# Routing tiles transposed by DMA during the readout, early gathers and weight loads in the routing block, query transposes on TensorE

## The chip, the cores and the metric

One core of one Trainium2 chip runs the whole program in one launch. The metric is the time of one execution on the device, in microseconds (us). Engines: TensorE (PE; PEld is its weight load), VectorE (DVE), ScalarE (ACT), GpSimd (POOL) and SyncE (SP). SP issues nearly all DMAs, POOL the casting and the indirect ones; 16 DMA engines move the data.

## The reference

The layer is a chain of four residual updates on x, shape (4, 512, 512), that is 2048 tokens of 512 features, with a context of (4, 1024, 512).

```python
x = x + tanh(g_xattn[0]) * xattn0(layernorm(x), ctx, mask)   # softmax(x ctx^T) ctx
x = x + tanh(g_ffn[0])   * ffn0(layernorm(x), router_w, wg, wu, wd)
x = x + tanh(g_xattn[1]) * xattn1(layernorm(x), ctx, Wq, bq, Wk, bk, Wv, bv, Wo, bo)   # 16 heads
x = x + tanh(g_ffn[1])   * ffn1(layernorm(x), w1, b1, w2, b2)   # 8 experts by position
```

`ffn0` picks for each token one of 8 experts by the argmax of 8 router logits. Each expert is three 512x512 products with ternary weights and with activations rounded to 8 bits: `down(square(relu(gate(x))) * up(x))`. The change touches the part between the end of the first update and the queries of the third.

## The kernel before, in words

The program is a row of blocks, each with one instruction list per engine; a block ends when every engine has finished its list, and the next one begins behind that barrier. Tokens are held as 16 tiles of 128 (`NT = 16`), four to a batch (`QD = 4`). A value of float32 precision is carried through TensorE as a pair of bf16 tiles, high and low part. "Turning" a pair means transposing its two 128x512 halves into eight 128x128 blocks, so that features lie on the partitions.

**Readout** (`readout_phase`, about 250 to 439 us): for each tile TensorE makes the scores of a later tile and the weighted sum of an earlier one. SP turns the pairs of x (L489) and of the probabilities (L495) by DMA transposes. From tile 5 on, DVE and ACT also do the routing work that does not need a finished batch ("route" of eleven tiles, `ROUTED_EARLY = 11`): the normalised tile is split into high (ACT, L541) and low part (DVE, L623) and quantised (ACT, L543) into a dispatch row.

**Routing** (`router_phase`, about 439 to 485 us): POOL zeroes a tile (L788), computes the reciprocal deviations (L789 to L791) and the padding (L792, L793), issues eight casting loads of the experts' ternary weights (L795), and then writes constants. SP loads the router's weights, then stores the dispatch rows to DRAM: eleven tiles when POOL's padding and DVE's first coefficients are there (L822), the other five when DVE and ACT have made them (L825, L827); it waits for the landing at L828 and L829. DVE normalises the five late tiles, TensorE turns all 16 tiles (L986) into PSUM, ACT copies each to SBUF (L845), TensorE makes the logits (L994). From the logits DVE (L915 to L975) computes each token's expert, and the list `token_of` (L968) that says which token stands in which row of 23 expert tiles.

**Mixture** (`mixture_phase`, to about 576 us): SP first loads the query and output weights (L1269). POOL gathers each expert tile's rows from DRAM (L1065) by `token_of`, four buffers deep; TensorE turns them (L1186) and runs the three products (L1202, L1217).

**Query** (`query_phase`, about 578 to 676 us): POOL gathers the mixture's rows back (L1331). Per batch DVE adds them (L1418), normalises four tiles (L1434, after POOL's deviations at L1337) and makes the low parts (L1439); ACT makes the high parts (L1394); SP turns the pairs by DMA (L1365); TensorE makes 4 groups of 12 matmuls (L1477); ACT (L1400) and DVE (L1444) take them out of PSUM, and SP stores them (L1373). SP's list is in this order: four pieces of the query weights and eight tiles turned; 32 loads of keys and values (L1251, L1254) for the attention block; then per batch four stores and four turns. The output weights are turned last. Attention follows at 676 us.

Of the kernel before, what the change touches and what calls it, by code (L numbers as in the profile page):

```python
# [6 lines left out]
F32 = mybir.dt.float32  # L7
# [409 lines left out]
RW = 2 * D + DW  # L417


def routed_views(flat):  # L420

    v = flat[:, 0:ROUTED_SHARED * RW].rearrange("p (t w) -> p t w", w=RW)
    return v[:, :, 0:2 * D].rearrange("p t (r d) -> p t r d", r=2), v[:, :, 2 * D:]


def readout_phase(nc, sem, mask, gates, ident, ctxN, ctxT, xres, moments, amax, routed):
# [4 lines left out]
    with ExitStack() as c:  # L431
# [19 lines left out]
        xpairs, disp = routed_views(routed)  # L451
# [28 lines left out]
        with nc.Block() as block:  # L480
            @block.sync
            def _(sp):
# [38 lines left out]
            def _(act):  # L521
# [15 lines left out]
                def route(r):  # L537
# [3 lines left out]
                    nc.scalar.copy(xpairs[:, r, 0, :], rxn[r % 2]).then_inc(rhi_done, 1)  # L541
# [18 lines left out]
            def _(dve):  # L560
# [43 lines left out]
                def route(r):  # L604
# [18 lines left out]
                    v.tensor_tensor(xpairs[:, r, 1, :], xn_r, xpairs[:, r, 0, :], ALU.subtract).then_inc(rlo_done, 1)  # L623
# [73 lines left out]
def router_phase(nc, sem, router_w, wt_dram, means, ident, xres, moments, amax, routed, wT, scales, expert_of, token_of, place, dispatch_dram):  # L697
# [5 lines left out]
    with ExitStack() as c:  # L703
# [9 lines left out]
        q32 = sb("r_q32", [P, 2, D], F32)  # L713
# [26 lines left out]
        chain = sem("r_chain")  # L740
# [37 lines left out]
        with nc.Block() as block:  # L778
            @block.gpsimd
            def _(pool):  # L780
# [6 lines left out]

                done(nc.gpsimd.memset(rows[:, :], 0.0))  # L788
                done(nc.gpsimd.memset(half[:, :], -0.5))  # L789
# [42 lines left out]
            def _(act):  # L832
# [8 lines left out]
                def x_copy(t):  # L841
                    act.wait_ge(xposed, t + 1)
                    if t >= 2:
# [5 lines left out]
                x_copy(0)  # L849
                act.wait_ge(router_xposed, 1)  # L850
                nc.scalar.copy(rT[:, :, :], psR[:, :, 0:E]).then_inc(router_ready, 1)
                for t in range(1, NT):
                    x_copy(t)
                    late = ROUTED_EARLY + (t - 3) // 2
                    if t >= 3 and t % 2 == 1 and late < NT:
                        high(late)
                        integers(late)

            @block.vector
            def _(dve):  # L860
# [107 lines left out]
                then(v.tensor_copy(token_of[:, :], psI))  # L968
# [1637 lines left out]
```

## Time and profile before

| | |
|---|---|
| time, median of 3 runs | 1586.51 us (1579.5 to 1591.86) |
| the profiled execution's own time | 1584.77 us |
| its span in the trace | 1583.0 us |
| TensorE busy, share of the span | 87% |
| VectorE | 70% |
| ScalarE | 57% |
| GpSimd | 33% |
| mean granted TensorE clock | 0.928 |

Times in rows are microseconds from the start of the span. A busy share is a mean over blocks that have different limits, so each block is read from its own stretch. "Idle before <- X" in a row names what the engine's idle time ended with.

### The profile page before, as it was taken

Reading aid. Unit: us, or ns where it says so; the run is one execution under the profiler, and the core shown is the slowest. Engines: PE = TensorE matmul, PEld = TensorE weight load, DVE = VectorE, ACT = ScalarE, POOL = GpSimd, SP = SyncE. Lnnn points to the kernel's source line nnn. Section 1 sums busy time; section 2 is a strip of 40 time slices with the busy share of each in tenths; the row PEclk is TensorE's granted clock in tenths of the full one; section 3 lists DMA queues with packets and bytes.
Section 4 is the critical chain, followed back from the end, with each engine's and each line's share of the span. In section 5 each row is a group of like instructions: output and inputs, shape, how many; then the busy total and the mean of one; then the engine's idle time right before and its main releaser. Section 6 shows DMA issues by size and latency. Waiting matters only on the chain. (4 is left out here: it accounts for less than half of the span.)

```text
span 1583.0 us, 25515 instructions
## 1 busy us (share of the span) xinstructions
PE 1369.5 (87%) x9345; PEld 813.7 (51%) x9415; DVE 1113.4 (70%) x1442; ACT 897.0 (57%) x1384; POOL 518.5 (33%) x412
## 2 busy tenths in 40 slices
PE   6899996999855945579999999999786999999996
PEld 4455552444342512216677777774233666666663
DVE  6888856677755968387888787875677766555561
ACT  7878842333353832307777777777434866656550
POOL 0122210000032324029999999997510000000000
PEclk9999998999966978759999999999897999999998
DMA  6888762533274459903353535352464965765540
GB/s 233 285 272 297 255 220 74 100 74 70 51 301 172 130 149 188 242 23 62 65 108 66 108 67 106 69 169 59 149 212 154 328 199 196 238 229 198 206 140 25
DMA packets 237166, 248.98 MB, mean 157 GB/s; under 512 B 121692, under 2 KB 154591, under 8 KB 236040
## 3 DMA queue, kind: packets, MB, share of 16 engines
q1 hardware_dynamic: 231224, 221.49, 49.2%
q0 software_dynamic: 5840, 26.14, 4.8%
q8 instruction: 63, 1.03, 0.3%
q14 instruction: 39, 0.32, 0.1%
HBM read 169.62 MB, written 52.59 MB: 140 GB/s over the span
## 5 line engine op out<-in xcount | busy, mean ns | idle before, releaser
L1726 POOL TENSOR_TENSOR t_low<-t_e 128x1024 bf16<-128x1024 f32 x185 | 365.1, 2003 | 47.7 <-ACT t_e L1773 47.6
L1811 DVE TENSOR_REDUCE t_nmax<-t_psM 128x1 f32<-128x1024 f32 x256 | 309.5, 1221 | 74.8 <-PE t_psM L1894 73.0
L1773 ACT ACTIVATE t_e<-t_psE 128x512 f32<-128x512 f32 x512 | 277.9, 595 | 104.5 <-PE t_psE L1916 97.3
L1894 PE MATMUL t_psM<-kst,qst 96*64 96x512 bf16 x1024 | 188.6, 405 | 13.9 <-DVE t_nmax L1811 7.0
L2435 PE MATMUL e_psG<-late_flat,e_w1p 128*128 (+1 forms) x1536 | 174.1, 277 | 13.1 <-DVE e_hT L2379 8.4
L1916 PE MATMUL t_psE<-qst,kst 99*64 99x512 bf16 x1024 | 181.7, 385 | 1.3
L2435 PEld LDWEIGHTS e_psG<-late_flat,e_w1p 128*128 128x128 bf16 x1536 | 152.2, 99 | 35.3 <-DVE e_hT L2379 8.0
L1930 PE MATMUL t_psO<-t_e,vst 128*33 128x512 bf16 x768 | 163.8, 391 | 3.7 <-POOL t_low L1726 3.7
L2450 PE MATMUL e_psO<-e_w2p,e_hT 128*128 128x512 bf16 x752 | 164.9, 379 | 0.8
L1894 PEld LDWEIGHTS t_psM<-kst,qst 96*64 96x64 bf16 x1024 | 88.8, 113 | 77.9 <-DVE t_nmax L1811 35.2
L2450 PEld LDWEIGHTS e_psO<-e_w2p,e_hT 128*128 128x128 bf16 x768 | 75.2, 98 | 88.8
L1930 PE MATMUL t_psO<-t_low,vst 128*33 128x512 bf16 x384 | 115.0, 380 | 0.0
L1916 PEld LDWEIGHTS t_psE<-qst,kst 99*64 99x64 bf16 x1024 | 80.6, 108 | 59.2 <-ACT t_e L1773 45.0
L120 POOL DMA_DIRECT2D ternary<-c_wout x48 | 41.8, 870 | 174.0 <-ACT c_wout L241 174.0
L669 PE MATMUL a_psS<-ctxT,a_xT 128*128 128x512 bf16 x375 | 86.6, 386 | 13.7 <-DMA a_xT<-a_xpair 13.0
L1477 PE MATMUL q_psG<-late_flat,q_wqT 128*128 128x512 bf16 x188 | 44.6, 398 | 53.9 <-DMA late_flat<-q_pair 50.9
L2331 ACT CAST e_w2p<-xres 128x2048 bf16<-128x2048 f32 x32 | 60.7, 1898 | 52.9 <-PE e_psO L2450 31.2
L376 PE MATMUL c_psG<-ctxT,c_wT 128*128 128x512 bf16 x369 | 86.6, 383 | 4.6 <-issue 2.7
L2337 ACT ACTIVATE e_g<-e_psG,e_b1T 128x256 f32<-128x256 f32 x128 | 53.6, 470 | 63.6 <-PE e_psG L2435 38.8
L1930 PEld LDWEIGHTS t_psO<-t_e,vst 128*33 128x33 bf16 x768 | 76.4, 109 | 23.1 <-POOL t_low L1726 4.7
L379 PE MATMUL c_psG<-c_wT,ctxT 128*128 128x512 bf16 x371 | 87.0, 384 | 0.7
L2371 DVE TENSOR_TENSOR e_w1p<-piece,e_w1p 128x2048 bf16<-128x2048 f32 x32 | 72.2, 2287 | 18.2 <-ACT e_w1p L2326 18.2
(270 smaller groups left out, 2212.7 us busy)
## 6 DMA issues: line engine op xcount, KB each, us to landing
piece<-in_L_ffn_w SPq DMA_DIRECT2D x32, 1024.0 KB, 13.9
xres<-in_L_ffn_w SPq DMA_DIRECT2D x32, 1024.0 KB, 15.2
wT<-ternary POOLq DMA_DIRECT2D x8, 1536.0 KB, 24.1
kst<-keys SPq DMA_DIRECT2D x96, 128.0 KB, 3.5
c_rows<-in_ctx SPq DMA_DIRECT2D x8, 1024.0 KB, 8.8
xres<-in_L_ffn_wg SPq DMA_DIRECT2D x8, 1024.0 KB, 6.0
xres<-in_L_ffn_wu SPq DMA_DIRECT2D x8, 1024.0 KB, 7.9
xres<-in_L_ffn_wd SPq DMA_DIRECT2D x8, 1024.0 KB, 6.4
```

Of the source, the lines that this page charges most:

```text
L376: last = nc.tensor.matmul(psG[:, k, :], wT[:, 0, a, k * P:(k + 1) * P], ctxT[:, b, q * 512:(q + 1) * 512], start=(i == 0), stop=(i == 11))
L379: last = nc.tensor.matmul(psG[:, k, :], ctxT[:, a, q * 512 + k * P:q * 512 + (k + 1) * P], wT[:, 1, b, :], start=(i == 0), stop=(i == 11))
L669: last = nc.tensor.matmul(psS[:, par, h * 512:(h + 1) * 512], xT[:, par, ra * KC + k, :], ctxT[:, rb * KC + k, bass.ds(b * T + h * 512, 512)],
L1726: nc.gpsimd.tensor_tensor(low[:, low_slot(h, u), :, :], e32[:, slot(h, u), :, :], upper(h, u), ALU.subtract).then_inc(lo_pool, 1)
L1773: nc.scalar.activation(e32[:, slot(h, u), i, :], psE[:, i, :], ACT.Exp, scale=SC).then_inc(expd, 1)
L1811: nc.vector.tensor_reduce(nmax[:, h // G % 2, h % G, u:u + 1], banks_of(place_of_max(b, m)).rearrange("p a t -> p (a t)"), AX_X, ALU.max, ...
L1894: last = nc.tensor.matmul(banks_of(place_of_max(b, m))[side * SIDE:(side + 1) * SIDE, i, :], qst[0:KR, g, h % G, s0:s0 + SIDE], kst[0:KR, ...
L1916: last = nc.tensor.matmul(psE[side * SIDE:(side + 1) * SIDE, i, :], kst[:, g, h % G, t0:t0 + SIDE], qst[:, g, h % G, :], start=True, stop= ...
L1930: return nc.tensor.matmul(psO[side * SIDE:side * SIDE + VW, h % 2, :], values(i, r), part[:, i, :], start=first, stop=last)
L2371: nc.vector.tensor_tensor(half1(1, p), raw1(p), half1(0, p), ALU.subtract).then_inc(w1_lo, 1)
L2435: last = nc.tensor.matmul(psG[:, g % 4, i, :], w1p[:, ra, k, f:f + P], xeT[:, rb * KC + k, ee, :].rearrange("p o s -> p (o s)"), start=(n ...
L2450: last = nc.tensor.matmul(psO[:, m, :], hT[:, ra, k, m * P:(m + 1) * P], w2p[:, rb, k, :], start=(k == 0 and i == 0), stop=(k == FC - 1 an ...
```

## The change

- The eleven early tiles are turned in the readout: their pairs now go into two buffers, and SP turns them by DMA (`turn_routed`) into the place where the pairs stood. ACT waits before it writes a pair's buffer until the turn of two tiles earlier has landed. In the routing block TensorE turns only the five late tiles, and ACT copies only those.
- POOL issues four of the eight weight loads directly behind its first memset, ahead of the deviations and the padding; the other four stay where they were.
- POOL issues the mixture's first four gathers at the end of the routing block, once the dispatch rows have landed and `token_of` is there. Their buffers share memory with the quantised tiles.
- In the query block all turns are done by TensorE into PSUM, eight transposes for one pair, and ACT copies the result to SBUF. TensorE's list holds one pair's transposes behind each group of 12 matmuls. SP's loads of keys and values wait for the first batch's update alone.

```diff
@@ readout_phase
+                def turn_routed(r):
+                    sp.wait_ge(rlo_done, r + 1)
+                    sp.dma_start_transpose(turned_of(rturned, r), rpairs[r % 2].rearrange("p r d -> p (r d)")).then_inc(r_turned[r % 2], 16)
...
                     if t + 1 < NT:
                         turn_p(t + 1)
+                    if 0 <= t - 6 < ROUTED_EARLY:
+                        turn_routed(t - 6)
+                turn_routed(ROUTED_EARLY - 1)
+                for i in range(2):
+                    sp.wait_ge(r_turned[i], (ROUTED_EARLY + 1 - i) // 2 * 16)
...
-                    nc.scalar.copy(xpairs[:, r, 0, :], rxn[r % 2]).then_inc(rhi_done, 1)
+                    if r >= 2:
+                        act.wait_ge(r_turned[r % 2], r // 2 * 16)
+                    nc.scalar.copy(rpairs[r % 2][:, 0, :], rxn[r % 2]).then_inc(rhi_done, 1)
@@ router_phase, POOL
                 done(nc.gpsimd.memset(rows[:, :], 0.0))
+                for e in range(E // 2):
+                    fetch(e)
                 done(nc.gpsimd.memset(half[:, :], -0.5))
...
-                for e in range(E):
-                    nc.gpsimd.dma_start(wT[:, e, :, :, :, :].rearrange("p m r k d -> p (m r k d)"),
-                                        wt_dram[e].rearrange("p m r k d -> p (m r k d)")).then_inc(w_fetched, 16)
+                for e in range(E // 2, E):
+                    fetch(e)
...
+                pool.wait_ge(early_stored, 16)
+                pool.wait_ge(late_stored, 32)
+                pool.wait_ge(q_cast, NT - ROUTED_EARLY)
+                pool.wait_ge(token_ready, 1)
+                for j in range(4):
+                    nc.gpsimd.indirect_dma_start(m_rows[:, j, :].bitcast(F32), None, dispatch_dram[:, :],
+                                                 bass.IndirectOffsetOnAxis(token_of[:, j:j + 1], 0)).then_inc(m_loaded[j], 16)
                 pool.wait_ge(w_fetched, 16 * E)
@@ router_phase, ACT
-                x_copy(0)
+                high(ROUTED_EARLY)
+                integers(ROUTED_EARLY)
                 act.wait_ge(router_xposed, 1)
                 nc.scalar.copy(rT[:, :, :], psR[:, :, 0:E]).then_inc(router_ready, 1)
-                for t in range(1, NT):
-                    x_copy(t)
-                    late = ROUTED_EARLY + (t - 3) // 2
-                    if t >= 3 and t % 2 == 1 and late < NT:
-                        high(late)
-                        integers(late)
+                for t in range(ROUTED_EARLY + 1, NT):
+                    high(t)
+                    integers(t)
+                    x_copy(t - 1)
+                x_copy(NT - 1)
@@ router_phase, TensorE
                 for t in range(NT):
-                    if t + 1 < NT:
+                    if t + 1 >= ROUTED_EARLY and t + 1 < NT:
                         x_transposes(t + 1)
                     judge(t)
@@ query_phase, SP
-                for n in range(NWT + 2 * QD):
-                    turn(n)
+                sp.wait_ge(updated, QD)
                 prefetch(sp)
...
-                    if b + 2 <= B:
-                        for k in range(QD):
-                            turn(NWT + (b + 2) * QD + k)
@@ query_phase, ACT
-                for n in range(NWT + 2 * QD):
+                for n in range(NWT):
+                    split(n)
+                    if n >= 2:
+                        copy(n - 2)
+                copy(NWT - 2)
+                copy(NWT - 1)
+                for n in tiles_of(0):
+                    split(n)
+                for n in tiles_of(0):
+                    copy(n)
+                for n in tiles_of(1):
                     split(n)
...
                         evacuate(b, k)
+                        copy(NWT + (b + 1) * QD + k)
                         if b + 2 <= B:
                             split(NWT + (b + 2) * QD + k)
@@ query_phase, TensorE
                     if m == 0:
-                        for i in range(4):
-                            pe.wait_ge(turned[i], (b + 2) * 16)
+                        pe.wait_ge(copied, NWT + (b + 1) * QD)
...
+                for n in range(NWT):
+                    transposes(n)
+                for n in tiles_of(0):
+                    transposes(n)
                 for b in range(B):
                     for m in range(KC):
                         gemm(b, m)
+                        transposes(NWT + (b + 1) * QD + m)
```

## Rows read from the trace of the kernel before

**Rows 1.** Busy time by stretch, readout: length, then each engine's busy time (count), clock, DMA.

```profile
300.00:325.00 25.00, 24.89 (x115) 11.37 (x116) 16.52 (x26) 7.61 (x11) 1.48 (x2) 1.00 0.44 82
```

**Rows 2.** Readout's transposes: timeline (start, length), then issues with us to landing.

```profile
394.08 33.33 SPq L495 DMA_TRANSPOSE a_pT<-a_ppair  x4
...
405.22 0.62 ACT L541 CAST late_flat<-ctxT 128x512 bf16<-128x512 f32 x1 [1.75 <-DVE ctxT L610]
...
437.53 0.75 DVE L597 SCALAR_TENSOR_TENSOR xres<-a_psR,a_coef,xres 128x512 f32<-128x512 f32 x1 [1.87 <-PE a_psR L681]
...
a_xT<-a_xpair SPq DMA_TRANSPOSE x16, 3.0
```

**Rows 3.** Timeline of the routing block, and of its groups of instructions the costliest.

```profile
440.10 0.11 POOL L789 MEMSET r_half<- 128x16 f32 x1
...
443.79 4.35 POOL L795 DMA_DIRECT2D wT<-ternary  x8
...
460.95 0.69 DVE L883 TENSOR_TENSOR r_xpair<-r_xn,r_xpair 128x512 bf16<-128x512 f32 x1 [2.17 <-ACT r_xpair L835]
...
466.63 0.29 DVE L915 TENSOR_REDUCE r_top<-r_psL 128x16 f32<-128x128 f32 x1 [4.45 <-PE r_psL L994]
...
480.80 0.18 DVE L968 CAST token_of<-r_psL 128x23 int32<-128x23 f32 x1
...
L845 ACT COPY r_xT<-r_psX 128x1024 bf16<-128x1024 bf16 x16 | 15.8, 1032 | 2.3 <-PE r_psX L986 2.3
```

**Rows 4.** DMA queues in 440:446, then 464:466 (packets, MB, share); SP's issue and wait.

```profile
q1 hardware_dynamic: 331, 0.34, 19.7%
...
q0 software_dynamic: 66, 0.76, 91.8%
q1 hardware_dynamic: 60, 0.06, 11.7%
...
462.63 0.48 SPq L827 DMA_DIRECT2D dispatch<-r_disp  x1
...
SPq L829 <- DMA dispatch<-r_disp: 21.6, 1, 21.6
```

**Rows 5.** Timeline at the start of the mixture block.

```profile
486.50 1.07 POOL L1065 DMA_INDIRECT m_rows<-dispatch,token_of  x1 [33.53 <-DVEq L1172]
...
490.40 0.95 POOL L1065 DMA_INDIRECT m_rows<-dispatch,token_of  x1 [0.31 <-issue]
...
493.19 0.61 PE L1186 MATMUL m_psX<-ident,m_rows 128*128 128x128 bf16 x4 [12.83 <-DMA m_rows<-dispatch,token_of]
```

**Rows 6.** Query block: timeline, one stretch (as rows 1), groups of ACT's instructions.

```profile
597.22 16.96 SPq L1365 DMA_TRANSPOSE late_flat<-q_pair  x8
...
636.10 4.38 SPq L1373 DMA_DIRECT2D queries<-q_qst  x4
...
617.77 1.91 DVE L1434 TENSOR_SCALAR q_xn<-xres,q_mom,q_rstd 128x512 f32<-128x512 f32 x4 [1.20 <-POOL q_rstd L1337]
...
631.94 1.91 DVE L1434 TENSOR_SCALAR q_xn<-xres,q_mom,q_rstd 128x512 f32<-128x512 f32 x4 [1.20 <-POOL q_rstd L1337]
...
620.49 10.52 PE L1477 MATMUL q_psG<-late_flat,q_wqT 128*128 128x512 bf16 x47 [2.65 <-DVE q_qst L1444]
649.09 1.86 PE L1477 MATMUL q_psG<-late_flat,q_wqT 128*128 128x512 bf16 x4 [18.08 <-DMA late_flat<-q_pair]
651.18 20.80 PE L1477 MATMUL q_psG<-late_flat,q_wqT 128*128 128x512 bf16 x90 [0.22 <-issue]
...
649.00:653.00 4.00, 3.69 (x9) 1.43 (x11) 1.82 (x3) 0.51 (x1) 0.00 (x0) 0.50 1.02 267
...
676.34 0.20 POOL L1745 MEMSET t_nparts<- 128x128 bf16 x1 [38.55 <-POOLq L1325]
...
L1400 ACT ACTIVATE q_qst<-q_psG,q_bias 128x512 bf16<-128x512 f32 x16 | 10.9, 686 | 36.7 <-DMA queries<-q_qst 23.5 <-PE q_psG L1477 13.2
L1394 ACT CAST q_pair<-q_xn 128x512 bf16<-128x512 f32 x16 | 9.3, 616 | 34.3 <-DVE q_xn L1434 16.9 <-issue 14.9 <-DMA late_flat<-q_pair 2.3
```

More of the change, by code:

```diff
@@ L450, in readout_phase @@
         stats = sb("a_stats", [P, NT, 6], F32)
-        xpairs, disp = routed_views(routed)
+        rturned, disp = routed_views(routed)
+        rpairs = [ctxT[:, 3 + i, 0:T].rearrange("p (r d) -> p r d", r=2) for i in range(2)]
         dead = lambda k: ctxT[:, k, 0:T].bitcast(F32)
@@ L694, in _, with router_phase @@
                 read(NT - 1, (NT - 1) % 2, B - 1)
-def router_phase(nc, sem, router_w, wt_dram, means, ident, xres, moments, amax, routed, wT, scales, expert_of, token_of, place, dispatch_dram):
+def router_phase(nc, sem, router_w, wt_dram, means, ident, xres, moments, amax, routed, wT, scales, expert_of, token_of, place, dispatch_dram, r_turned, m_rows, m_loaded):
     NS = NT + E - 1
@@ L739, in router_phase @@
         tokens_ready, columns_ready = sem("r_tokens_ready"), sem("r_columns_ready")
[L740 removed]
+        chain, token_ready = sem("r_chain"), sem("r_token_ready")
         iota_e = sb("r_iota_e", [P, NS, E], F32)
@@ L967, in _ @@
                 dve.wait_ge(inverted, 1)
-                then(v.tensor_copy(token_of[:, :], psI))
+                v.tensor_copy(token_of[:, :], psI).then_inc(token_ready, 1)
                 then(v.tensor_tensor(mine[:, :, :], iota_e[:, :, :], owner[:, :, :].to_broadcast([P, NS, E]), ALU.is_equal))
@@ L1022, in _, with mixture_phase @@
                 last.then_inc(inverted, 1)
-def mixture_phase(nc, sem, ident, wT, scales, expert_of, token_of, dispatch_dram, mixture_dram, prefetch):
+def mixture_phase(nc, sem, ident, wT, scales, expert_of, token_of, dispatch_dram, mixture_dram, prefetch, rows, loaded):
     NS = NT + E - 1
@@ L1047, in mixture_phase @@
         psY = c.enter_context(nc.psum_tensor("m_psY", [P, 2, D], F32))
-        loaded = [sem(f"m_loaded{i}") for i in range(4)]
         xposed = sem("m_xposed")
@@ L1061, in _ @@
             def _(pool):
-                for j in range(NS):
+                for j in range(4, NS):
                     pool.wait_ge(xposed, j + 1)
@@ L1301, in query_phase @@
         hi_done, lo_done = sem("q_hi_done"), sem("q_lo_done")
-        turned = [sem(f"q_turned{i}") for i in range(4)]
+        xposed = sem("q_xposed")
+        copied = sem("q_copied")
         gemm_done = sem("q_gemm_done")
@@ L1467, in _, with transposes @@
             def _(pe):
+                def transposes(n):
+                    pe.wait_ge(lo_done, n + 1)
+                    if n >= 2:
+                        pe.wait_ge(copied, n - 1)
+                    for r in range(2):
+                        for k in range(KC):
+                            last = nc.tensor.transpose(psX[:, n % 2, r * KC + k, :], pair[:, n % 4, r, k * P:(k + 1) * P],
+                                                       ident[:, :])
+                    last.then_inc(xposed, 1)
                 def gemm(b, m):
                     if m == 0:
-                        for i in range(4):
-                            pe.wait_ge(turned[i], (b + 2) * 16)
+                        pe.wait_ge(copied, NWT + (b + 1) * QD)
                     if b > 0:
@@ L2506, in flamingo_kernel @@
         flat_rows = flat[:, :].bitcast(BF16).rearrange("p (t r d) -> p t r d", r=2, d=D)
+        r_turned = [sem(f"r_turned{i}") for i in range(2)]
         with ExitStack() as early:
@@ L2534, in flamingo_kernel @@
                 token_of = moe.enter_context(nc.sbuf_tensor("token_of", [P, NT + E - 1], mybir.dt.int32))
+                m_rows = moe.enter_context(nc.sbuf_tensor("m_rows", [P, 4, DW], BF16))
+                m_loaded = [sem(f"m_loaded{i}") for i in range(4)]
                 router_phase(nc, sem, a["L0_ffn_router_w"], wt_dram, means, ident, xres, moments, amax, flat[:, :].bitcast(BF16),
-                             wT, scales, expert_of, token_of, place, dispatch_dram)
-                mixture_phase(nc, sem, ident, wT, scales, expert_of, token_of, dispatch_dram, mixture_dram, prefetch_query_weights)
+                             wT, scales, expert_of, token_of, place, dispatch_dram, r_turned, m_rows, m_loaded)
+                mixture_phase(nc, sem, ident, wT, scales, expert_of, token_of, dispatch_dram, mixture_dram, prefetch_query_weights,
+                              m_rows, m_loaded)
             nc.clear_and_free_semaphores(used)
```

54 lines of the change are left out of this document (31 added, 23 removed).

## Prediction, made before the run

> **What bounds the kernel now.** Blocks follow each other behind barriers, so the change is priced block by block: first the busy time by stretch, then each block's timeline, then the DMA queues and SP's waits. The chain of waits for the whole run lies in the last blocks, which the change does not touch; what is won before them shifts them as they are.
>
> *Readout.* TensorE is busy 24.89 of 25 us and makes 115 matmuls of 512 columns, 0.216 us each, at the full clock level of 2.4 GHz [rows 1]. DMA share is 0.44 there. This block is TensorE's; at its end DVE's update waits 1.87 us for TensorE's last sum [rows 2].
>
> *Routing.* Three things end close together: DVE's `token_of` at 480.98, its scales soon after, and the landing of the late dispatch stores. SP issued these until 463.1 and waited 21.6 us, to 484.7 [rows 4]. That wait is the last. The reason is in the queue rows: in 464:466 the casting loads hold 91.8% of the 16 engines and SP's stores 11.7%, with 66 and 60 packets [rows 4]. The DMA engines are full, so this block ends when loads and stores together are through. TensorE's 16 turns and ACT's 16 copies (15.8 us) [rows 3] stand beside that.
>
> *Start of the mixture.* The first gather is issued at 486.50, 1.8 us behind SP's release, and TensorE's first transpose starts at 493.19, on the gather's landing [rows 5].
>
> *Query.* SP is the bound. Its eight turns end at 614.18, the 32 loads of keys and values behind them at 636.10, and only then come the stores and the turns of batch 2; TensorE waits 18.08 us for these turns and starts that batch at 649.09 [rows 6].
>
> **The change, part by part.**
>
> *Eleven turns in the readout: 0.* SP's issue of a probability turn (the row's four end at 427.41) leaves TensorE 9 us or more to the next; one more DMA transpose of x's size lands 3.0 us after its issue [rows 2]. It stands behind `turn_p` in SP's list and its low part is a step old, so SP waits for nothing new. Queued behind it: the next `turn_x`, some 5 us later. ACT's new wait is for the turn of two tiles before. With the turn of tile r-2 issued behind that of 394.08, at about 396, and landing at 399 to 400, ACT's copy at 405.22 [rows 2] finds it done with 5 us to spare; behind ACT there wait DVE's low part and the next step. If that cover were gone, the delay would be paid in each of nine steps. In the last step several turns follow each other, but DVE's 1.87 us and the final update lie over them. Bounds: 0 to +2.
>
> *Routing: compute.* Four load issues now stand ahead of POOL's deviations: 4 x 4.35/8 = 2.2 us [rows 3], and DVE starts that much later; the padding and so the early store too. DVE's last low part ended at 461.64, after a wait of 2.17 for ACT [rows 3], which no longer has the old copies in front: 461.64 + 2.2 - 2.17 = 461.7. Behind it: eight transposes (at most twice the 0.61 of four, [rows 5]), a copy of 1.03, twelve small matmuls, together 2.7, so the argmax starts at 464.4 in place of 466.63, and `token_of` is there at 478.8. SP's late stores can go at about 462, as before. This 2.2 us, all that eleven turns less bring here, is not what ends the block.
>
> *Routing: DMA.* The first loads are issued at 440.10 in place of 443.79 [rows 3], 3.7 us earlier. Before, the stores ran alone ahead of the loads with 19.7% of 6 us [rows 4], 1.2 us of all engines, and that lead goes. With the engines full from then on, the same work ends 3.7 - 1.2 = 2.5 us earlier, at 482.2. Bounds: 3.7 earlier (481.0), or 2.2 later (486.9) if the early store's own start decides. I take 482.2, since the two shares sum to 103% [rows 4].
>
> *First gathers.* POOL waits for that landing and `token_of`, then issues four in 491.35 - 486.50 = 4.85 us [rows 5]. Behind them on POOL stands only the block's end, for which all engines wait: 482.4 + 4.85 + the 1.8 us of the barrier = 489.0. By the landing it is the same: 482.4 + 6.7 (486.50 to 493.19) = 489.1; I expect less, as the weights' prefetch comes behind these gathers now. TensorE's first transpose moves from 493.19 to 489.0: **-4.2 us**. Bounds: -7.6 (if only `token_of` at 478.8 decides) to +0.6 (486.9 + 0.2 + 4.85 + 1.8 = 493.8).
>
> *Query.* DVE's normalising of batch 2 at 617.77 and of batch 3 at 631.94 hang on POOL and DVE [rows 6], not on SP; they are the anchors. SP's loads start with the first update, which is before the first turn of a tile at 597.22 [rows 6], and take 636.10 - 614.18 = 21.9 us of SP: they are through by 619.1 at the latest, before the first store wants SP at about 620. Each pair costs ACT a copy more, 1.03 us [rows 3] beside an evacuation of 0.69 and a split of 0.62 [rows 6]. Behind an anchor (0.6 later, when the first tile is there) ACT goes through one split, then three times evacuation and copy, with two splits between: 0.62 + 3 x 1.72 + 1.24 = 7.0 us. Batch 1 so starts at 618.4 + 7.0 = 625.4, 4.9 later than 620.49 [rows 6]; that delays nothing at the end, as batch 2 waits for its own anchor. The split that was late moves batch 3's normalising by about 1 us, to 632.9, and the last copy of batch 2 ends at 632.9 + 7.0 = 639.9: TensorE starts batch 2 at 640.0 in place of 649.09, 9.1 earlier. From there eight groups of 12 x 0.216 = 2.59 us, with seven sets of eight transposes between, 0.43 each (128 columns, a quarter of 0.216, an estimate from [rows 1]): 23.7, and 1.3 for the copy at the batch boundary: the end is 665.0 in place of 651.18 + 20.80 = 671.98, -7.0. Before, these groups began at the lower level: 0.50 granted in 649:653, nine matmuls in 3.69 us [rows 6]; ten such cost 2 us more. The new gap ahead of batch 2 is about 3 us, near the 2.65 us after which 47 matmuls took 10.52 us at full pace, far from the 18.08 that brought the lower level [rows 6], so mostly no charge. I take **-6.0 us**, a microsecond off for steps between engines. Bounds: -2 (SP's stores or a gather late) to -8. SP's earlier loads share the DMA engines with POOL's gathers; DVE's updates would wait for that, and the bound of -2 holds it.
>
> *Sum*: 0 - 4.2 - 6.0 = -10.2. The profiled execution took 1584.77 us for a span of 1583.0, 1.7 under the median of 1586.51: 1584.77 - 10.2 = **1574.6**.
>
> **A rule weighed.** In 464:466 the two queues moved 66 and 60 packets, about one for one, though a load's packet is some ten times as large [rows 4]. The Trainium skill (DMA: Bandwidth & Descriptors, section Queues, rings and completion order) says that each DMA engine goes round-robin between the queue rows that have work, packet by packet; the trace agrees. By that rule alone earlier loads cannot hasten the stores, since the stores get their turn at the same pace until the loads are through; it speaks against the early half of the loads, and by it the first term would be about -2 in place of -4.2 (rival 1). The same skill (VectorE: DVE Perf Modes, section Rules for kernel authors) advises TensorE for a 128x128 transpose where PSUM may be the target and DMA otherwise, which speaks against the first part; by it the readout would lose nothing here either, because rows 1 have TensorE full and the DMA engines not.
>
> **Rivals.**
> 1. *The stores, not the total, decide.* They start 2.2 later, alternate one for one, and land at 484.7 as before. Then 484.9 + 4.85 + 1.8 = 491.5, -1.7, sum -7.7: 1577. For: the packet counts. Against: the full engines. 0.2.
> 2. *The query block gives nothing*: the keys' loads, now beside the gathers, end after the first store wants SP, and ACT's evacuations wait for stores as before. Sum -4.2: 1580.6. For: SP bounded this block. Against: the 619.1 above is a latest time. 0.13.
> 3. *More than forecast*: the stores land at the earliest bound and `token_of` decides (-7.6), and the query's best case (-8): 1569. 0.14.
> 4. *Slower: TensorE stays at the lower clock in the query block.* It now waits for a copy at each batch, and groups are broken by transposes. Place: batches 2 and 3; price: 96 matmuls x (0.41 - 0.216) = +18.6 on top of -10.2, so +8.4: 1593. It decides if the granted clock at a gap of 3 us falls and does not come back. Against: 2.65 us did not lower it, and within a batch no gap is left. 0.05.
> 5. *The readout pays.* If a routed turn lands more than 9 us after its issue, ACT's copy waits in each of nine steps; at 12 us that is +27 less 10: 1601. Against: 3.0 us to landing. 0.03.
>
> **How the numbers follow.** My forecast, both gains near their size, gets 0.45: 1569 to 1580 by itself. The runs shown scatter by 6 us to each side. The range 1563 to 1586 takes in rivals 1 to 3 and the bounds with that scatter, and leaves out 4 and 5. About 1% (16 us) is what can be told from no change here: faster by more needs rival 3 or the forecast at its edge: 0.2. Slower by more needs rival 5, or 4 with scatter: 0.04. Within: 0.76.
>
> **What would show it.** Right: TensorE's first mixture transpose 3 to 6 us earlier against the readout's end; four gathers issued inside the routing block; POOL's wait before them ending on the dispatch landing; readout steps unchanged in length; in the query block no wait for a DMA turn, batch 1's matmuls later and batch 2's about 9 us earlier against the block's start. Wrong: ACT's L541 copy waiting for a DMA in the readout; the stores landing as late as before; a query clock of 0.5 in the last two batches; attention's start less than 4 us earlier relative to the query block's own start.

## The result, and the profile after

The changed kernel took 1574.31 us (median of 7 runs, 1574.06 to 1576.73), the kernel before 1583.38 (7 runs, 1579.5 to 1591.86): a ratio of 0.9929, 95% interval 0.991 to 0.9948. That is faster by 0.7%, inside the 1% that the prediction could not tell from no change, and at 1574.3 against a forecast of 1574.6. The profiled span fell from 1583.0 to 1573.2 us.

A block's length is the time from its first POOL instruction to the next block's; "routing" ends with TensorE's first mixture transpose. So read, the two profiled executions differ as follows (us):

| stretch | before | after | difference | forecast |
|---|---|---|---|---|
| before the readout (not changed) | 250.9 | 248.4 | -2.5 | 0 |
| readout | 188.61 | 190.13 | +1.5 | 0 |
| routing, to the first mixture transpose | 53.67 | 48.92 | -4.75 | -4.2 |
| mixture | 84.93 | 84.21 | -0.7 | 0 |
| query | 98.22 | 91.75 | -6.5 | -6.0 |
| attention (not changed) | 457.11 | 458.17 | +1.1 | 0 |
| the rest (not changed) | 449.55 | 451.61 | +2.1 | 0 |

Over all fourteen profiles the first row scatters by 6 us (247.3 to 253.4) and the last by 3 (449.5 to 452.4), though the code there is the same, so single executions are compared from readout to attention's start: 425.43 and 415.01 us, 10.4 less.

**Readout after.** One stretch in its middle answers to [rows 1]: length, then busy time and count of PE, PEld, DVE, ACT and POOL, granted clock, DMA share, GB/s. The second row is the block's last 13 us.

```profile
299.00:324.00 25.00, 25.00 (x118) 11.36 (x116) 15.56 (x23) 8.30 (x12) 1.48 (x2) 1.00 0.41 77
...
425.50:438.50 13.00, 7.85 (x24) 2.89 (x24) 9.35 (x25) 1.88 (x3) 0.00 (x0) 0.74 0.53 100
```

Its timeline (start, length, engine and line, idle time before), answering to [rows 2]:

```profile
403.27 0.62 ACT L558 CAST ctxT<-ctxT 128x512 bf16<-128x512 f32 x1 [1.75 <-DVE ctxT L627]
404.21 2.06 SPq L506 DMA_TRANSPOSE late_flat<-ctxT  x1
...
417.84 5.35 PE L698 MATMUL a_psR<-ctx_more,a_pT 128*128 128x512 bf16 x24 [2.27 <-DMA a_pT<-a_ppair]
428.60 7.85 PE L698 MATMUL a_psR<-ctx_more,a_pT 128*128 128x512 bf16 x24 [5.40 <-DMA a_pT<-a_ppair]
429.98 0.62 ACT L558 CAST ctxT<-ctxT 128x512 bf16<-128x512 f32 x1 [3.09 <-DMA late_flat<-ctxT]
```

TensorE is as full as before in the middle, and ACT's copy at 403.27 waits 1.75 us for DVE exactly as the one at 405.22 did: the turns cost nothing in the steady steps. Only the last copy waits for a DMA turn. The end differs. These are the same two groups of 24 matmuls in the kernel before (one record is missing from the trace):

```profile
419.74 7.04 PE L681 MATMUL a_psR<-ctx_more,a_pT 128*128 128x512 bf16 x24 [2.16 <-DMA a_pT<-a_ppair]
430.39 7.04 PE L681 MATMUL a_psR<-ctx_more,a_pT 128*128 128x512 bf16 x23 [3.61 <-DMA a_pT<-a_ppair]
```

The last 24 matmuls now wait 5.40 us for their turn instead of 3.61, but the turn is not later: the group ahead of them took 5.35 us instead of 7.04, so TensorE was there sooner. From start to start the two groups lie 10.76 us apart after and 10.65 before, so the wait itself cost 0.1 us. The last group then takes 7.85 us instead of 7.04, with a granted clock of 0.74 in the last 13 us instead of 0.87. That is 0.8 of the readout's 1.5 us; the other 0.6 had come before these two groups.

**Routing after.** Timeline and ACT's copies, answering to [rows 3] and [rows 5]:

```profile
439.37 2.24 POOL L806 DMA_DIRECT2D wT<-ternary  x4 [0.30 <-POOL r_rows L809]
445.40 2.23 POOL L806 DMA_DIRECT2D wT<-ternary  x4
461.11 8.34 SPq L856 DMA_DIRECT2D dispatch<-r_disp  x1
462.91 0.29 DVE L944 TENSOR_REDUCE r_top<-r_psL 128x16 f32<-128x128 f32 x1 [2.26 <-PE r_psL L1028]
477.12 0.18 DVE L997 CAST token_of<-r_psL 128x23 int32<-128x23 f32 x1
479.74 1.07 POOL L838 DMA_INDIRECT m_rows<-dispatch,token_of  x1 [27.01 <-DMA dispatch<-r_disp]
483.64 0.95 POOL L838 DMA_INDIRECT m_rows<-dispatch,token_of  x1 [0.30 <-issue]
487.46 0.58 PE L1217 MATMUL m_psX<-ident,m_rows 128*128 128x128 bf16 x4 [10.78 <-ACTq L1147]
...
L874 ACT COPY r_xT<-r_psX 128x1024 bf16<-128x1024 bf16 x5 | 5.0, 1008 | 3.9 <-PE r_psX L1015 3.9
```

ACT copies five tiles where it copied 16. `token_of` is there at 477.12, 38.6 us into the block, and the landing of the stores still releases POOL later, as before. SP's last wait (line, what it waited for, us in total, times, longest) and the DMA queues, answering to [rows 4]; the queue rows (packets, MB, share of the 16 engines) are 463:465 and then 474.54:476.54:

```profile
SPq L858 <- DMA dispatch<-r_disp: 9.4, 1, 9.4
...
q0 software_dynamic: 76, 0.76, 93.5%
q1 hardware_dynamic: 68, 0.07, 13.0%
...
q1 hardware_dynamic: 663, 0.66, 106.4%
```

While the casting loads last, SP's stores get about one packet for each of theirs (68 and 76 in 2 us), as they did before. When the loads are through, the same queue moves 663 packets in 2 us, ten times as many. The stores therefore end soon after the loads do, and the loads now fill the engines within the first 5 us of the block. By stretches of 5 us from the block's start, before (first, second and ninth):

```profile
439.52:444.52 5.00, 1.77 (x18) 1.36 (x19) 1.82 (x5) 1.74 (x3) 4.71 (x8) 0.70 0.01 3
444.52:449.52 5.00, 4.80 (x84) 4.36 (x84) 3.17 (x10) 3.62 (x5) 4.78 (x11) 0.61 0.97 287
...
479.52:484.52 5.00, 0.60 (x16) 0.50 (x16) 3.57 (x14) 0.00 (x0) 0.00 (x0) 0.50 0.49 185
```

and after (first, second and eighth):

```profile
438.54:443.54 5.00, 1.04 (x8) 0.77 (x8) 0.95 (x3) 0.62 (x1) 4.52 (x8) 0.70 0.61 237
443.54:448.54 5.00, 0.32 (x12) 0.32 (x13) 3.14 (x7) 1.72 (x4) 4.79 (x10) 0.50 1.04 428
...
473.54:478.54 5.00, 1.18 (x32) 1.01 (x32) 4.73 (x13) 0.00 (x0) 0.00 (x0) 0.50 0.71 227
```

The share in the first 5 us rose from 0.01 to 0.61, and the last partly filled stretch is the eighth instead of the ninth. The bytes are the same, 14.8 MB up to those two stretches.

**Query after.** Timeline, one stretch and a group, answering to [rows 6]; the block starts at 571.67 (before: 578.12).

```profile
581.30 2.71 SPq L1282 DMA_DIRECT2D kst<-keys  x6
610.77 1.06 SPq L1285 DMA_DIRECT2D vst<-values  x2
614.52 19.55 SPq L1399 DMA_DIRECT2D queries<-q_qst  x8
618.68 4.10 PE L1525 MATMUL q_psG<-late_flat,q_wqT 128*128 128x512 bf16 x12 [3.32 <-ACT late_flat L1422]
633.85 2.76 PE L1525 MATMUL q_psG<-late_flat,q_wqT 128*128 128x512 bf16 x12 [1.51 <-ACT late_flat L1422]
656.53 2.75 PE L1525 MATMUL q_psG<-late_flat,q_wqT 128*128 128x512 bf16 x12
...
611.67:621.67 10.00, 5.10 (x24) 2.10 (x22) 8.98 (x15) 6.65 (x10) 3.98 (x4) 0.83 0.78 185
...
L1428 ACT ACTIVATE q_qst<-q_psG,q_bias 128x512 bf16<-128x512 f32 x16 | 11.1, 691 | 16.4 <-PE q_psG L1525 16.4
```

SP's loads end at 611.83 and its first store leaves at 614.52. ACT's evacuations no longer wait for stores (23.5 us before), and TensorE waits for ACT's copies, 3.32 us at most, where it waited 18.08 us for DMA turns. Batch 2 starts 62.2 us into the block, where it had started at 71.0.

### The profile page after: what moved, and what is told of

Same layout as the page of the kernel before. It is cut to its first block and busy times, and to the rows that moved or that the text cites. A ratio compares the mean times of both kernels' runs of the same rounds, so it can differ in the third digit from the quotient of the medians.

```text
span 1573.2 us, 25795 instructions
## 1 busy us (share of the span) xinstructions
PE 1383.8 (88%) x9519; PEld 822.2 (52%) x9519; DVE 1114.2 (71%) x1442; ACT 909.5 (58%) x1397; POOL 518.1 (33%) x412
## 5 line engine op out<-in xcount | busy, mean ns | idle before, releaser
L376 PE MATMUL c_psG<-ctxT,c_wT 128*128 128x512 bf16 x384 | 91.0, 390 | 3.7 <-issue 2.7
L2432 DVE TENSOR_TENSOR e_hT<-e_g,e_hT 128x512 bf16<-128x512 f32 x64 | 43.7, 690 | 54.9 <-ACT e_hT L2393 54.9
## 6 DMA issues: line engine op xcount, KB each, us to landing
xres<-in_L_ffn_w SPq DMA_DIRECT2D x32, 1024.0 KB, 14.8
```

The source lines that it names most:

```text
L376: last = nc.tensor.matmul(psG[:, k, :], wT[:, 0, a, k * P:(k + 1) * P], ctxT[:, b, q * 512:(q + 1) * 512], start=(i == 0), stop=(i == 11))
```

## The experiments

All experiments are timed against the kernel before on the same chip. "Gathers" is the time from routing's start to the first mixture gather, "routing" that to the first mixture transpose. For reading: gathers 46.98 before and 41.20 after; routing, readout, query and attention as in the table above.

**The two halves alone.**

```diff
 e1: the changed kernel with the query block of before
 e2: the kernel before with the query block of the changed one
```

> The readout, routing and mixture parts of the change, with the query block of before. My theory (two gains that add up): from the routing block's first memset to the mixture's first transpose 48.9 us, as in the changed kernel, against 53.7 before; query block 98.2 us as before; time about 5 us under the kernel before. Rival (the readout pays for its eleven DMA transposes what routing wins): the readout is 1.5 us longer and the time is only 3 to 4 us under. Rival (the time won comes from the query block alone): within 1 us of before.

Measured: 1584.16 against 1586.82 us, ratio 0.9985 (0.9966 to 1.0003). In the profile routing 49.01, query 99.67, readout to attention's start 421.95.

> The query part of the change alone, everything else as before. My theory: query block 91.8 us against 98.2 before, time about 6.5 us under; batch 2's matmuls start on ACT's copy and not on a DMA. Rival (the query block gains only because its rows and weights come earlier from the routing change): under 2 us won.

Measured: 1579.44 us, ratio 0.9965 (0.9945 to 0.9985). Query 91.85, routing 53.95, readout to attention's start 419.33.

The two halves bring 3.5 and 6.1 us in the profile, 9.6 together against 10.4: they add up, and neither hides the other. The rival of e2 falls, as the query block gains as much without the routing change. The first half brings nothing that its timed interval can tell from none: its 4.7 us in routing are partly paid back in the readout (189.27) and in the query block (99.67 against 98.22, with the same code there; why is open).

**Which part of routing.**

```diff
 e3 (router_phase, POOL)
-                for e in range(E // 2):
-                    fetch(e)
...
-                for e in range(E // 2, E):
+                for e in range(E):
 e4: the four gathers back in the mixture block
-                pool.wait_ge(early_stored, 16)
...
-                for j in range(4):
-                    nc.gpsimd.indirect_dma_start(m_rows[:, j, :].bitcast(F32), None, dispatch_dram[:, :],
...
```

> The changed kernel with all eight weight loads behind the padding again, so POOL's deviations and the early store have their old lead. My theory (the DMA engines are full, and what starts earlier ends earlier): the late stores land 2.5 to 4 us later after the block's first memset than the 41.2 us of the changed kernel, time 2.5 to 4 us over the changed kernel. Rival (the queues alternate packet for packet, the stores decide, and the early half of the loads brings nothing): landing at 41 us or earlier, time equal to the changed kernel or up to 2 us less.

Measured: ratio 0.9958 (0.9942 to 0.9975). Gathers 45.92, routing 53.59, against 46.98 and 53.67 before. The first gather and SP's wait in it:

```profile
483.13 1.07 POOL L836 DMA_INDIRECT m_rows<-dispatch,token_of  x1 [32.55 <-DMA dispatch<-r_disp]
...
SPq L856 <- DMA dispatch<-r_disp: 22.4, 1, 22.4
```

Without the early half the wait is again 22.4 us (21.6 in [rows 4]) and the whole routing gain is gone, although eleven turns less and the early gathers are still there. What fewer turns and earlier gathers save is not seen here, because the landing still comes last.

> The changed kernel with the first four gathers back in the mixture block. Theory A (the gain of the routing block is that its stores land earlier; four gathers of 4.85 us hold the block open nearly as long as they save): first gather about 2 us after the landing, 6.7 us more to the first transpose, 49.6 us after the block's first memset against 48.9, time 0.5 to 1 us over the changed kernel. Theory B (the early gathers are what wins): 53 us, time 4 us over.

Measured: ratio 0.9945 (0.9924 to 0.9966). Gathers 43.02, routing 49.39, mixture 84.71 against 84.21. The early gathers bring 0.5 us in routing. The 0.5 in the mixture is not shown, as other kernels with early gathers lie at 84.0 to 85.0. The early loads bring the rest.

**Order of loads and stores.**

```diff
 e7 (router_phase, POOL)
                 done(nc.gpsimd.memset(rows[:, :], 0.0))
+                nc.gpsimd.memset(disps[:, :, D + 2:DW], 0.0).then_inc(pads_set, 1)
+                nc.gpsimd.memset(disp_late[:, :, D + 2:DW], 0.0).then_inc(pads_set, 1)
                 for e in range(E // 2):
```

> The changed kernel with POOL's two padding memsets ahead of the first four loads, so that the early store can start about 3 us sooner. Theory A (the DMA engines are full from the first load on, and the order of the work in them does not matter): first gather 41.2 us after the block's first memset, within 0.5; time equal within 1 us. Theory B (packets alternate and the stores' own start sets their end): first gather 38 to 40 us, time 1 to 3 us under the changed kernel.

Measured: 1572.9 against 1587.14 us, ratio 0.9912 (0.9889 to 0.9935). Gathers 41.13 against 41.20, routing 48.89 against 48.92. The early store leaves 3 us earlier into the block (442.47 for 445.50, with starts at 438.55 and 438.54) and nothing ends sooner: the early store's own start does not decide.

**Turning by DMA in the readout.**

```diff
 e5: readout and routing turns as before; early loads, early gathers and new query block kept
-                    if 0 <= t - 6 < ROUTED_EARLY:
-                        turn_routed(t - 6)
...
-                    if t + 1 >= ROUTED_EARLY and t + 1 < NT:
+                    if t + 1 < NT:
                         x_transposes(t + 1)
```

> The changed kernel with the eleven routing tiles turned by TensorE in the routing block again (readout as before, loads and gathers of the change kept). Theory A (with the stores landing 41.2 us after the block's first memset, ACT's eleven copies and the 2.2 us of load issues would put token_of last): first gather at about 43.8 us, first mixture transpose 2.6 us later than in the changed kernel; readout 0.7 to 1.5 us shorter; time 1 to 2 us over the changed kernel. Theory B (the stores decide with or without the turns): first gather at 41.2 us, time 0.7 to 1.5 us under the changed kernel.

Measured: 1577.26 us, ratio 0.9932 (0.9912 to 0.9953). Routing 50.17 (1.25 more than the changed kernel), readout 188.48 (1.65 less), readout to attention's start 415.06 against 415.01. In its routing block POOL's first gather waits for DVE's `token_of`, not for the landing; in its readout the last group waits 3.69 us, as it did before (3.61):

```profile
482.92 1.07 POOL L826 DMA_INDIRECT m_rows<-dispatch,token_of  x1 [28.21 <-DVE token_of L985]
...
431.54 6.17 PE L686 MATMUL a_psR<-ctx_more,a_pT 128*128 128x512 bf16 x21 [3.69 <-DMA a_pT<-a_ppair]
```

So the eleven DMA turns bring 1.25 us in routing, about half of what theory A said, and the timed ratio (0.9932 against 0.9929) cannot tell the two kernels apart. What the turns cost is less clear. With them eleven profiles put the readout at 188.4 to 190.1 (mean 189.6), without them three at 188.5 to 188.65. The wait is not the price. In e9 it is as long as in the changed kernel, and yet the readout took only 188.38:

```profile
430.53 6.64 PE L698 MATMUL a_psR<-ctx_more,a_pT 128*128 128x512 bf16 x23 [5.42 <-DMA a_pT<-a_ppair]
```

The length goes with the clock granted in the last 13 us. It was 0.87 in the five profiles at 188.4 to 188.65 (before, e2, e5, e9, e12) and 0.74 in the nine at 189.3 to 190.1. All nine have the DMA turns, but e9 and e12 run the very same readout code, so the code alone does not decide it. What sets this clock was not found, and it stays open whether the turns have a price of their own.

**Why the query block got shorter.**

```diff
 e6 (query_phase, SP)
-                sp.wait_ge(updated, QD)
+                sp.wait_ge(lo_done, NWT + 2 * QD)
                 prefetch(sp)
 e11: query block of before, with the loads ahead of the tiles' turns
                 for n in range(NWT):
                     turn(n)
+                sp.wait_ge(updated, QD)
                 prefetch(sp)
                 for n in range(NWT, NWT + 2 * QD):
                     turn(n)
```

> The changed kernel with SP's 32 loads of keys and values waiting until batch 1's low parts are made, about where they stood in the kernel before. Theory A (SP's list bounds the block, so the place of these loads is half of the gain): batch 0's stores wait for them, ACT's evacuations of batch 1 wait for the stores, query block about 96 to 97 us against 91.8, time 4 to 5 us over the changed kernel. Theory B (taking the turns off SP is the whole gain): query block 92 us, time equal.

Measured: 1580.37 us, ratio 0.9958 (0.9939 to 0.9977). Query 99.27, longer than before, with TensorE turning all tiles. Its timeline:

```profile
605.38 3.96 SPq L1282 DMA_DIRECT2D kst<-keys  x6
627.83 14.74 SPq L1399 DMA_DIRECT2D queries<-q_qst  x8
633.92 0.69 ACT L1428 ACTIVATE q_qst<-q_psG,q_bias 128x512 bf16<-128x512 f32 x1 [13.81 <-DMA queries<-q_qst]
```

The loads begin at 605.38, the first store waits behind them until 627.83, and ACT's evacuation waits 13.81 us for that store.

> The changed kernel's routing, mixture and early key and value loads, with the query block's transposes taken back to DMA on SP's queue as before: weight turns, then the loads at once when the first four tiles are updated, then the turns of the tiles. Theory (the gain of the query block needs both: the loads moved ahead, and the tile turns off their queue): the turns of the first tiles now stand behind 32 load issues and beside their data, and the query block takes 95 to 101 us against 91.75 (changed) and 98.2 (before). Rival (the place of the loads is the whole gain, and which engine turns the tiles is worth nothing): 91 to 93 us.

Measured: 1592.57 against 1587.52 us, ratio 1.0038 (1.002 to 1.0055): slower than before. Query 105.71, beyond even the theory's 101. Its timeline:

```profile
615.59 13.67 SPq L1396 DMA_TRANSPOSE late_flat<-q_pair  x8
622.70 0.69 DVE L1473 TENSOR_TENSOR q_pair<-q_xn,q_pair 128x512 bf16<-128x512 f32 x1 [17.01 <-ACT q_pair L1428]
626.18 21.99 PE L1511 MATMUL q_psG<-late_flat,q_wqT 128*128 128x512 bf16 x94 [55.36 <-DMA late_flat<-q_pair]
```

The turns of the first eight tiles leave at 615.59, behind all 32 loads; pair buffers come free late, DVE waits 17.01 us and TensorE 55.36. The rival (the loads' place is the whole gain) falls. Both parts are needed: the loads early, and the turns off SP's queue so that they can be. DMA turns issued from another engine's queue were not run, so it is not shown that it has to be TensorE.

**What bounds the query block now.**

```diff
 e8 moves only deviations(0) ahead; e10 (query_phase, POOL):
-                for t in range(NR):
+                for t in range(2 * QD):
                     gather(t)
                 pool.wait_ge(half_set, 1)
                 deviations(0)
-                for t in range(NR, NT):
+                for t in range(2 * QD, 3 * QD + 2):
+                    gather(t)
+                deviations(1)
+                for t in range(3 * QD + 2, NT):
                     gather(t)
                 for b in range(B):
-                    if b >= 1:
+                    if b >= 2:
                         deviations(b)
+                    pool.wait_ge(rstd_ready, max(b + 1, 2))
```

> The changed kernel with POOL's first reciprocal deviations behind eight gathers in place of twelve. Theory A (the query block now hangs on DVE's chain of updates and normalisings, which starts with POOL's deviations): they come 3.7 us earlier, all later anchors with them, query block 88 us against 91.8, time 3 to 4 us under the changed kernel. Theory B (SP's loads of keys and values, or the later gathers, bound it next): query block over 90.5 us, time less than 1.5 us under.

Measured: 1576.94 us, ratio 0.9936 (0.9916 to 0.9957), query 93.84. The first normalising came at 583.03, 12.0 us into the block instead of 16.8 (588.43 - 571.67), so 4.7 us earlier; the 5.4 in the next expectation leaves out that the blocks start 0.7 apart. But the second waited for POOL, which had gathers and a memset of 3.51 us ahead of the second deviations:

```profile
584.91 3.26 POOL L1364 DMA_INDIRECT q_rows<-mixture,place  x1 [0.30 <-issue]
...
600.74 1.46 DVE L1473 TENSOR_SCALAR q_xn<-xres,q_mom,q_rstd 128x512 f32<-128x512 f32 x3 [7.38 <-POOL q_rstd L1370]
```

> The changed kernel with POOL's list in the query block in another order: 8 row gathers, the reciprocal deviations of batch 0, 6 gathers, the deviations of batch 1, 2 gathers, and only then the memsets (in the changed kernel: 12 gathers, deviations 0, 4 gathers, a memset of 3.5 us, deviations 1). Theory (VectorE's normalising, which waits for POOL's deviations, sets the pace of the query block): the first normalising comes 5.4 us earlier, as with the deviations moved alone, and the second now follows it, at about 594.5 on the changed kernel's clock instead of 600.1; the query block takes 86 to 88 us instead of 91.75. Rival 1 (the bound behind it is TensorE and ScalarE at the half clock, or the late rows of the gathers): the batches come earlier but wait there, 89.5 to 92. Rival 2 (gathers stand beside the key and value loads, which start earlier by as much, and their issues slow down): 92 to 94.

Measured: 1571.0 against 1587.52 us, ratio 0.9897 (0.9857 to 0.9936). Query 87.48, 4.3 less than the changed kernel. The second normalising of the changed kernel, whose block starts at 571.67:

```profile
600.07 1.92 DVE L1473 TENSOR_SCALAR q_xn<-xres,q_mom,q_rstd 128x512 f32<-128x512 f32 x4 [1.24 <-POOL q_rstd L1370]
```

The first two normalisings of e10, the block starting at 574.85:

```profile
586.88 1.92 DVE L1477 TENSOR_SCALAR q_xn<-xres,q_mom,q_rstd 128x512 f32<-128x512 f32 x4 [1.23 <-issue]
...
598.38 2.10 DVE L1477 TENSOR_SCALAR q_xn<-xres,q_mom,q_rstd 128x512 f32<-128x512 f32 x4 [1.17 <-POOL q_rstd L1370]
```

The second now begins 23.5 us into the block instead of 28.4 (600.07 - 571.67) and waits 1.17 us for POOL. The theory holds: once SP no longer bounds the block, DVE with POOL's deviations does.

**Two gathers instead of four.**

```diff
 e9
-                for j in range(4):
+                for j in range(2):
                     nc.gpsimd.indirect_dma_start(m_rows[:, j, :].bitcast(F32), None, dispatch_dram[:, :],
...
-                for j in range(4, NS):
+                for j in range(2, NS):
```

> The changed kernel with only the first two mixture gathers in the routing block; the other two come back to the mixture block, ahead of gathers 4 and up. The four gathers in routing take POOL 0.95 us and a gap of 0.3 us each (479.74 to 484.6), and the routing block ends behind them. Theory (the block is held open by POOL's list, not by what the gathers carry): two gathers less let the mixture block begin about 2.5 us earlier, and the stretch from the start of routing to the first mixture transpose comes out at 46.5 to 47.5 us instead of 48.9, the span 1.5 to 2.4 us shorter. Rival (the first transposes wait for the rows of gathers 0 and 1 and for the weights, whichever block they stand in): the stretch stays at 48.5 to 49.5, and what follows can be longer by the late gathers 2 and 3, so the mixture block 84.2 to 86.

Measured: 1576.74 us, ratio 0.9922 (0.9892 to 0.9951). Routing 46.22, 2.7 less, so the theory's first step holds: POOL's list keeps the block open. But the mixture took 87.97, 3.8 more. Its TensorE:

```profile
485.48 0.59 PE L1217 MATMUL m_psX<-ident,m_rows 128*128 128x128 bf16 x4 [7.87 <-ACTq L1147]
...
493.18 0.40 PE L1217 MATMUL m_psX<-ident,m_rows 128*128 128x128 bf16 x4 [1.74 <-DMA m_rows<-dispatch,token_of]
```

The third tile's rows now come behind the weights' prefetch, and TensorE waits 1.74 us for them where it had waited for none. That is under half of the 3.8; the rest was not followed. Routing and mixture together are 1.1 us longer than in the changed kernel, so the shorter span that the theory forecast did not come. The four early gathers are worth their place because of what follows them in the DMA queues.

**Both orders together.**

```diff
 e12: the edits of e7 and of e10
```

> The changed kernel with POOL's list in the query block in the new order (8 gathers, deviations 0, 6 gathers, deviations 1, 2 gathers, memsets) and the pads of the dispatch rows set ahead of the first loads in routing. Theory (the pads' place is worth nothing, as the DMA engines work through the same bytes by the same time, and the query order is worth its 4.3 us beside all else): query block 87 to 88 us, routing up to the first gather 41.0 to 41.4, 1570 to 1572 us and a ratio of 0.989 to 0.992 against the kernel before. Rival (the 1.4 us by which the pads' kernel was below the changed one is real and adds up): a ratio of 0.987 to 0.989.

Measured: 1570.4 us (5 runs, 1569.88 to 1574.67) against 1588.38, ratio 0.9901 (0.9882 to 0.9919). Gathers 41.15, so the pads' place is again worth nothing, and the rival's sum is not seen. The profiled execution, the slowest of the five, has a query block of 89.24; one row of POOL and one of DVE show a loss that e10 did not have:

```profile
608.38 3.51 POOL L1387 MEMSET kst<- 3x4096 bf16 x1
...
609.42 2.50 DVE L1470 TENSOR_SCALAR q_veps<-q_mom 128x4 f32<-128x4 f32 x1
```

e10 and e12 have the lowest medians here; between them nothing can be told. Their medians lie about 3 to 4 us under that of the changed kernel, but the intervals of the ratios overlap (0.9857 to 0.9936 and 0.9882 to 0.9919 against 0.991 to 0.9948).

## Why the prediction was right

- **Total.** 1574.6 forecast, 1574.3 measured. It is partly luck: the terms of the changed stretch sum to -10.4 against -10.2, but the mixture's -0.7 was not forecast, and two small losses (readout, attention) and scatter outside the change (-2.5 and +2.1) also had to cancel. The forecast also starts from one profiled execution, 1584.77; from the result's median of the kernel before, 1583.38, the same -10.2 gives 1573.2.
- **Readout, 0.** Right for the nine steady steps, and rival 5 fell with them. The whole came to +1.5, inside the bounds of 0 to +2, but not for the reason that the bounds allowed for: the turns that follow each other there held the last group of matmuls back by 0.1 us, while the clock of that group, which the term does not price, took 0.8.
- **Routing, compute.** `token_of` was put 39.3 us into the block (478.8 - 439.52) and came at 38.6; it did not end the block. e5 shows what it hid: without DMA turns `token_of` is the last.
- **Routing, DMA.** The mechanism held, its size was too small. A landing 2.5 us earlier was forecast; measured from the block's start it went from 45.2 (484.7 - 439.52) to 40.3 (461.11 + 8.34 + 9.4 - 438.54), 4.9 earlier. The sum took the loads' 3.7 us and subtracted 1.2 for the stores' lead. The stores did run alone (260 packets in 445.02:446.02 before, at a share of 0.96), but at 270 GB/s, where stretches full of loads and stores move 397 to 428. Counted in bytes, by the rows above, 3.3 MB are through in the first 10 us after and 1.45 MB before; at 415 GB/s that is an estimated 4.5 us of the 4.9.
- **First gathers.** Four issues from 479.74 to 484.59, 4.85 us as taken. But the first left 0.9 us behind the landing (479.74 - 478.85) where 0.2 was taken, and from the last TensorE needed 2.87 us where 1.8 was taken. These 1.8 us ate up most of the 2.4 by which the landing was put too late, so that -4.75 for -4.2 is two misses that nearly cancel: luck.
- **The rule weighed in the text.** The Trainium skill (DMA: Bandwidth & Descriptors, section Queues, rings and completion order) says round-robin by packet, and the trace after agrees (76 and 68 packets). Rival 1 drew from it that the stores would land as late as before, and fell: the rule gives the pace while both queues have work, not the end of the stretch, which the total of bytes gives.
- **Query, -6.0.** Right in the steps of TensorE, counted from the block's start: batch 1 forecast at 47.3 and measured at 47.0, batch 2 at 61.9 and 62.2, the end of the matmuls at 86.9 and 87.6. Rivals 2 and 4 fell; e6 and e11 show that the loads' place and the free SP queue make the gain only together. One detail failed: batch 1's first group, behind a gap of 3.32 us, took 4.10 us instead of 2.75 at a granted clock of 0.83 in its stretch, so such a gap was charged. Batch 2's was 1.51 and took 2.76. It cost nothing, as batch 2 hangs on its own normalising. One cost was too low: SP's 32 loads took 30.5 us (581.30 to 611.83) where 21.9 was taken. They began only 9.6 us into the block and so ended at 40.2, just inside the latest time of the sum (619.1, or 41.0) and 2.7 us before the first store; rival 2 fell by that much.
- **Not foreseen.** Attention, whose code is the same, took 1.1 us more. With the new query block and its early loads (after, e2 to e5, e7 to e10, e12) it took 458.2 to 458.7 us, with the old block, or with late loads in e6, 456.2 to 457.1; e11, old block with early loads, took 458.0. So it goes, as far as single profiles show, with the early loads and not with the engine that turns: between e6 and the changed kernel, which differ in the loads' place alone, it is 2.0 us. One place where it shows is 30 to 60 us into the block, before and after:

```profile
706.34:736.34 30.00, 29.52 (x226) 17.49 (x228) 23.54 (x20) 20.55 (x39) 23.89 (x17) 0.92 0.08 16
```

```profile
693.42:723.42 30.00, 29.69 (x224) 17.73 (x226) 23.37 (x20) 20.30 (x39) 23.68 (x17) 0.89 0.07 14
```

The granted clock there is 0.89 instead of 0.92; why is open.

## What to carry to other kernels

Where a stretch keeps the DMA engines full, fill them earlier: the head start counts (e3), while a store that was let go 3 us sooner inside the stretch ended no sooner (e7). A DMA turn on a queue that also carries long loads ties the two together; taking the turns to another engine pays only if the loads then really move (e6, e11). When one bound is gone, look at once for the next engine's instruction order: POOL's list was then worth 4.3 us (e10), about as much as the whole first half of this change in its own block.

## What the hardware showed that was not expected

- An issue on SP can itself be held: the late dispatch store took 8.34 us to issue (461.11), 0.48 before [rows 4]. Casting loads filled the engines both times. What differs is how far SP's queue had come with its first store: from that store's issue to the late one's it moved 332 packets after and 1177 before. In e7, with 444 packets, the issue took 5.46 us. That the store ahead in the same queue holds the issue fits these numbers and is not shown. It delayed nothing, as SP had only waits behind it.
- POOL and DVE held each other up in two places. In e12 a DVE instruction on 128x4 elements took 2.50 us instead of 0.17 and ended at 611.92, just behind POOL's memset (608.38 + 3.51 = 611.89). In e8 a gather's issue took 3.26 us instead of 0.95, beside four subtractions of DVE from 584.86 to 587.35. The Trainium skill (SBUF — State Buffer, section SBUF: two separate sides) says that the two engines share one port pair, which in the cases it lists one of them holds for a whole instruction. The first pair of rows agrees to 0.03 us, and the second fits, though in the changed kernel gathers beside such subtractions took 0.95 and 1.25.
- TensorE's clock at the end of the readout was granted at 0.74 or 0.87 in kernels with the same instructions there, and the last 24 matmuls took 7.85 or 6.64 us accordingly (after, e9), both behind a wait of 5.4 us.
